# Two edits in a four-stage image kernel: ScalarE takes the first expert and a later copy; residual tiles are loaded, and partly added, during the first sweeps

## The reference, cut to what matters

```python
x = x + dynamic_conv(gn(x))   # 3x3, weights mixed for each sample from 4 experts by a softmax
x = x + scnn_1(gn(x))         # four sweeps of 63 dependent steps
x = x + attention(gn(x))      # linear attention with rotation, plus a 3x3 depthwise conv
x = x + scnn_3(gn(x))         # four sweeps again

# dynamic_conv, for a sample
g = mean(x, (2, 3));  alpha = softmax(relu(g @ w1.T + b1) @ w2.T + b2)
weff = sum_k alpha[k] * experts[k];  out = conv3x3(x, weff) + sum_k alpha[k] * bias[k]

# one sweep (down, up, right, left): row i needs row i - 1
new = row + relu(conv1d(prev, w, b))      # 9 taps, 64 channels to 64
```

## Time and profile before

| what | value |
| --- | --- |
| device time, median of 3 runs | 3130.79 us (3127.74 to 3137.73) |
| the profiled execution's own time | 3132.45 us |
| span of its trace | 3130.7 us |
| mean granted TensorE clock | 0.945 |
| busy: PE, DVE, ACT, POOL | 88%, 69%, 44%, 9% |
| dynamic convolution | 0 to 429 us |
| first sweeps | 429 to 1339 us |
| local part | 1339 to 1583 us |
| attention | 1583 to about 2180 us |
| second sweeps, final sum | to 3067 us, to the end |

### The profile page before, as it was taken

The page is one execution under the profiler, slowest core; times in us unless marked ns, Lnnn a source line. Parts: engine busy times, 40 slices in busy tenths (PEclk is TensorE's granted clock), DMA queues, the critical chain, the costliest instruction groups (busy, mean ns, idle before and its releaser), DMA issues. The chain is left out here.

```text
span 3130.7 us, 71818 instructions
## 1 busy us (share of the span) xinstructions
PE 2747.3 (88%) x25712; PEld 2482.8 (79%) x25712; DVE 2172.1 (69%) x5174; ACT 1363.0 (44%) x2113; POOL 288.4 (9%) x801
## 2 busy tenths in 40 slices
PE   5888879999999999917969998878999999999791
PEld 3666669999999999913447777758999999999791
DVE  7888846666666666687018888886666666666865
ACT  3766642246632222236436666643225662222120
POOL 1112110000000000045000101010000000000602
PEclk9899989999999999958979999998999999999795
DMA  4334230000000000087054877856000000000758
GB/s 89 81 90 99 67 124 0 0 0 0 0 0 0 0 0 0 0 233 198 1 87 73 120 104 102 116 73 107 0 0 0 0 0 0 0 0 0 121 94 127
DMA packets 735622, 164.89 MB, mean 53 GB/s; under 512 B 728209, under 2 KB 728849, under 8 KB 730641
## 3 DMA queue, kind: packets, MB, share of 16 engines
q1 hardware_dynamic: 608928, 136.86, 22.7%
q10 hardware_dynamic: 126576, 26.41, 5.4%
HBM read 96.13 MB, written 67.11 MB: 52 GB/s over the span
## 5 line engine op out<-in xcount | busy, mean ns | idle before, releaser
L269 PE MATMUL L_conv<-L_x_hi,L_w_hi 128*128 128x256 f32 x5040 | 1251.0, 283 | 46.5 <-DVE L_w_lo L236 28.7
L269 PE MATMUL L_conv<-L_x_hi,L_w_lo 128*128 128x256 f32 x5040 | 1249.5, 283 | 0.0
L156 ACT ACTIVATE L_row_b<-S,L_bias 128x256 f32 (+1 forms) x1008 | 514.2, 510 | 1168.9 <-DVE L_x_hi L210 1158.0
L269 PEld LDWEIGHTS L_conv<-L_x_hi,L_w_hi 128*128 128x128 f32 x5040 | 958.7, 190 | 49.5 <-issue 28.9
L269 PEld LDWEIGHTS L_conv<-L_x_hi,L_w_lo 128*128 128x128 f32 x5040 | 957.0, 190 | 0.0
L220 DVE SCALAR_TENSOR_TENSOR S<-L_conv,L_neg_bias,L_row_b 128x256 f32 x1008 | 487.7, 484 | 517.5 <-PE L_conv L273 516.7
L273 PE MATMUL L_conv<-L_x_lo,L_w_hi 128*128 128x256 f32 x5040 | 771.3, 284 | 4.9 <-DVE L_x_lo L212 4.8
L273 PEld LDWEIGHTS L_conv<-L_x_lo,L_w_hi 128*128 128x128 f32 x5040 | 677.7, 190 | 7.4 <-DVE L_x_lo L212 7.4
L212 DVE TENSOR_TENSOR L_x_lo<-S,L_x_hi 128x256 fp32r<-128x256 f32 x1016 | 455.3, 448 | 34.7
L210 DVE TENSOR_SCALAR L_x_hi<-S 128x256 fp32r (+1 forms) x1016 | 316.7, 312 | 35.3
L604 PE MATMUL dc_conv<-dc_xz_hi,dc_w_hi 128*128 128x512 f32 x384 | 171.3, 446 | 6.5 <-DVE dc_w_lo L731 6.5
(11 more groups left out here) (177 smaller groups left out, 2896.4 us busy)
## 6 DMA issues: line engine op xcount, KB each, us to landing
dc_raw<-x SPq DMA_DIRECT2D x32, 512.0 KB, 6.6
x_scratch<-dc_raw SPq DMA_DIRECT2D x16, 1024.0 KB, 7.4
lp_xr<-x_scratch SPq DMA_DIRECT2D x16, 1024.0 KB, 7.0
x_scratch<-lp_xr SPq DMA_DIRECT2D x32, 512.0 KB, 7.7
at_res<-x_scratch SPq DMA_DIRECT2D x32, 512.0 KB, 10.5
x_scratch<-at_res SPq DMA_DIRECT2D x64, 256.0 KB, 5.3
fs_buf<-x_scratch SPq DMA_DIRECT2D x32, 512.0 KB, 6.7
at_G<-x_scratch ACTq DMA_DIRECT2D x56, 256.0 KB, 5.8
```

The source lines that it names most:

```text
L156: nc.scalar.activation(row_b[p][:, :, :], line(k, at_step(k, i), p), ACT.Identity, bias=bias[:, k:k + 1]).then_inc(row_b_ready[p], 1)
L269: nc.tensor.matmul(out, w[:, k, s * P:(s + 1) * P], x_hi[p][:, s:s + J, :], start=(s == 0 and n == 0), stop=False)
```

## The change

**In the dynamic convolution.**
- ACT's fourth copy of a sample into S (`ph` 1, `pw` 1) no longer stands behind the third, but one sample later, behind `evacuate` of the last chunk.
- The product of expert 0 with its weight goes from DVE to ACT (`first_expert`), behind `exps`; `centre` z = 1 now stands ahead of `exps`. Two semaphores are new: `weight_ready` (DVE to ACT), `first_mixed` (ACT to DVE).
- DVE's `remainder` z = 1 goes from behind the mixing to between `mixing_weights` and the mixing.
- At the start, the two expert loads go from ACT's queue to SP's, behind the first sample; low weights of sample 0 are made ahead of its remainders and of the statistics of sample 1; PE does the products of chunks 0 and 1 of sample 0 ahead of the group average of sample 1. At the end, DVE does three of the last four copies and ACT one.

**Behind it.** A class `Shared` owns five tiles of 1 MB. SP loads the x1 of samples 0 to 4 into them in the first sweeps. In the fourth direction POOL adds to each three quarters of S (three times 5 additions of 128x32x16), and DVE takes their 15 statistics between the halves of 15 steps that are written out; the loop of 63 steps becomes four loops and these 15 steps. In the local part only a quarter is left to add for these samples. The band tiles (6 MB) are now loaded on ACT's queue at the start of the local part, and PE waits for them in four parts. SP now loads a sample ahead of storing the next. At the end of the local part, SP loads the constants and the first two `G` tiles into the same five tiles (DVE sets only their edge columns to one), so that the attention starts without these loads, and without the two memsets.

The core of the diff:

```diff
@@ sweeps, DVE @@
-                with dve.Fori(0, STEPS) as i:
-                    for p in range(2):
-                        step(k, dve.snap(i), p)
+                if k == 3 and final:
+                    final.early_vector(dve, step)
+                else: ...
@@ dyn_conv, ACT, sample @@
                     evacuate(n * CH - 1, (k - 1) % PER, CH - 1, n - 1)
+                if not first and not second:
+                    to_slot(n - 2, (k - 2) % PER, 1, 1)
                 if not last:
                     centre(t, k + 1, 0)
                 evacuate(n * CH, k % PER, 0, n)
                 if not last:
                     hidden(n + 1)
+                    centre(t, k + 1, 1)
                     exps(n + 1)
-                    centre(t, k + 1, 1)
+                    first_expert(n + 1)
                 evacuate(n * CH + 1, k % PER, 1, n)
@@ dyn_conv, DVE, sample @@
                     mixing_weights(n + 1)
-                    for e in range(KE):
+                    remainder(n + 1, k + 1, 1)
+                    for e in range(1, KE):
                         mix(n + 1, (k + 1) % 2, e)
...
-                    remainder(n + 1, k + 1, 1)
                     low_weights(n + 1, (k + 1) % 2)
@@ Shared @@
+    def early_pool(self, pool, new_ready, done_before):
+        for n in range(RING):
+            pool.wait_ge(self.x1_in[n], 16)
+        for g in (3, 2, 1):
+            for p in range(2):
+                pool.wait_ge(new_ready[p], done_before(3, STEPS - g * QUARTER))
+            for n in range(RING):
+                self.add_quarter(self.nc.gpsimd, n, g).then_inc(self.quarter_summed, 1)
+    def early_vector(self, dve, step):
...
+        for g in (3, 2, 1):
+            ready = STEPS - g * QUARTER + RING + 1
+            several(at, ready)
+            for n in range(RING):
+                step(3, ready + n, 0)
+                dve.wait_ge(self.quarter_summed, (3 - g) * RING + n + 1)
+                self.quarter_stats(n, g).then_inc(self.early_stats, 1)
+                step(3, ready + n, 1)
+            at = ready + RING
+        several(at, STEPS)
@@ local_part @@
             for n in range(B):
                 sp.wait_ge(x2_ready, n + 1)
+                if n >= 2 and n - 2 + RING < B:
+                    sp.wait_ge(x2_stored[(n - 2) % RING], 32 * ((n - 2) // RING + 1))
+                    sp.wait_ge(normed, n - 1)
+                    shared.load_residual(sp, n - 2 + RING)
                 for q in range(2): ...
+            shared.load_constants(sp, *constants)
+            sp.wait_ge(pads_ready, 4)
+            shared.load_normalised(sp, x2, 0, 0)
+            shared.load_normalised(sp, x2, 1, 1)
@@ local_part, ACT and PE @@
+            bands.load(act)
...
-            pe.wait_ge(bands.loaded, 8 * 16)
             pe.wait_ge(normed, NB)
             for w in range(W):
+                if w % 16 == 0:
+                    pe.wait_ge(bands.loaded[w // 16], 2 * 16)
@@ attention @@
-            for t in G:
-                nc.vector.memset(t[:, :, :], 1.0).then_inc(set_up, 1)
```

More of the change, by code:

```diff
@@ L466, in store @@
                              raw[u][:, :, :].rearrange("p i w -> p (i w)")).then_inc(x1_stored, 16)
-            for n in range(PER):
+            load(0, 0)
+            sp.dma_start(ex[0], halves(experts[:, 0, :])).then_inc(ex_in, 16)
+            sp.dma_start(ex_rest[:, :, :], experts[:, 1:KE, :]).then_inc(ex_in, 16)
+            for n in range(1, PER):
                 load(n, n)
@@ L545, in high_weights, with to_slot @@
                 nc.scalar.copy(halves(w_hi[u][:, :]), w_mix).then_inc(w_hi_ready, 1)
-            def to_slot(n, u, ph):
+            def to_slot(n, u, ph, pw):
                 act.wait_ge(affine_ready, n + 1)
-                for pw in range(2):
-                    dst, src, scale, shift = slot_move(n, u, u % 2, ph, pw)
-                    nc.scalar.activation(dst, src, ACT.Identity, bias=shift, scale=scale).then_inc(s_done, 1)
+                dst, src, scale, shift = slot_move(n, u, u % 2, ph, pw)
+                nc.scalar.activation(dst, src, ACT.Identity, bias=shift, scale=scale).then_inc(s_done, 1)
             def sample(t, k):
@@ L625, in sample @@
                 first, last = isinstance(n, int) and n == 0, isinstance(n, int) and n == B - 1
+                if first:
+                    for q in range(2):
+                        products_high(0, q, 0, 0)
+                        products_high(0, q, 0, 1)
+                        products_low(0, q, 0)
+                    group(1, INP)
+                    products_high(0, 2, 0, 0)
+                    products_high(0, 2, 0, 1)
+                    products_low(0, 2, 0)
+                    hid(1)
+                    products_high(0, 3, 0, 0)
+                    logits(1)
+                    products_high(0, 3, 0, 1)
+                    products_low(0, 3, 0)
+                    return
                 if not last:
@@ L633, in sample @@
                 products_high(n, 1, u, 0)
-                if not first:
-                    group(n - 1, RES)
+                group(n - 1, RES)
                 if not last:
@@ L801, in _ @@
             gate_hidden(0)
-            remainder(0, 0, 0)
             softmax_in(0)
-            remainder(0, 0, 1)
+            mixing_weights(0)
+            dve.wait_ge(ex_in, 2 * 16)
+            for e in range(1, KE):
+                mix(0, 0, e)
+            low_weights(0, 0)
+            for z in range(2):
+                remainder(0, 0, z)
             for q in range(CH):
@@ L820, in _ @@
             dve.wait_ge(affine_ready, B)
-            for pw in range(2):
-                dst, src, scale, shift = slot_move(B - 1, (B - 1) % PER, (B - 1) % 2, 1, pw)
+            for ph, pw in ((0, 1), (1, 0), (1, 1)):
+                dst, src, scale, shift = slot_move(B - 1, (B - 1) % PER, (B - 1) % 2, ph, pw)
                 nc.vector.tensor_scalar(dst, src, scale, shift, ALU.mult, ALU.add)
@@ L831, in __init__, with load @@
         self.band1 = ctx.enter_context(nc.sbuf_tensor("lp_band1", [P, W, HALF], F32))
[L832 to L834 removed]
+        sem = semaphores(nc, ctx, "lpb")
+        self.loaded = [sem(f"loaded{g}") for g in range(4)]
+    def load(self, eng):
         for g in range(4):
             part = slice(g * 16, g * 16 + 16)
[L837 to L838 removed]
@@ L845, with local_part @@
 GROUP_EVERY = 7
 NORM_LAG = 8
-def local_part(nc, ctx, S, bands, affine, x1, x2, group_avg, lepe_b):
+def local_part(nc, ctx, S, bands, affine, shared, x2, group_avg, lepe_b, constants):
     def sb(name, shape, dt=F32):
@@ L854, in local_part @@
     sem = semaphores(nc, ctx, "lp")
-    xr = [sb(f"xr{u}", [P, J, W]) for u in range(RING)]
+    xr, x1_in = shared.xr, shared.x1_in
     avg = sb("avg", [P, P])
@@ L1002, in _ @@
                 if n < B:
-                    mark = front(n)
+                    sums = front(n)
                 if n >= 2:
@@ L1008, in _, with attention @@
                 if n < B:
-                    middle(n, mark)
+                    middle(*sums)
+            dve.wait_ge(normed, B)
+            for u in range(RING):
+                dve.wait_ge(x2_stored[u], 32 * len(range(u, B, RING)))
+            for pad in shared.pads():
+                nc.vector.memset(pad, 1.0).then_inc(pads_ready, 1)
 HEADS, HD = 8, 8
 ROWS = 8
-def attention(nc, ctx, S, affine, x2, x3, consts, rotations, wq_in, wk_in, bq_in, bk_in):
+def attention(nc, ctx, S, affine, shared, x2, x3):
     def sb(name, shape, dt=F32):
@@ L1021, in attention @@
     sem = semaphores(nc, ctx, "at")
-    G = [sb(f"G{u}", [P, J // 2, 2 * W + 2]) for u in range(2)]
-    T = [sb(f"T{u}", [P, J // 2, P]) for u in range(2)]
+    G, rot, cst, wq, wk, b_raw, y = shared.G, shared.rot, shared.cst, shared.wq, shared.wk, shared.b_raw, shared.y
+    g_in, consts_in = shared.g_in, shared.consts_in
+    T = [sb("T0", [P, J // 2, P]), shared.turned]
     res = [sb(f"res{u}", [P, C, J]) for u in range(2)]
@@ L1701, in early_sync, with early_vector, early_pool @@
             self.load(sp, item)
-    def early_pool(self, pool, new_ready, count):
+    def early_vector(self, dve, step):
+        with dve.Fori(0, STEPS) as i:
+            for p in range(2):
+                step(3, dve.snap(i), p)
+    def early_pool(self, pool, new_ready, done_before):
         for p in range(2):
-            pool.wait_ge(new_ready[p], count)
+            pool.wait_ge(new_ready[p], done_before(3, STEPS - PART))
         for item in range(B):
```

214 lines of the change are left out of this document (126 added, 88 removed).

## The result

| kernel | median | runs |
| --- | --- | --- |
| before | 3130.81 us (3126.49 to 3137.73) | 20 |
| changed | 3138.36 us (3132.24 to 3151.82) | 20 |

The ratio of the changed kernel to the one before is 1.0029, with a 95% interval of 1.0021 to 1.0037: slower by 7.5 us by the medians and 9 by the ratio, where 5.8 us faster was forecast. The time lies in the range, but on the other side of no change. The profiled execution's span is 3137.2 us against 3130.7, mean clock 0.941 against 0.945.

The account below looks back on a forecast made before the run. PE bounds the sweeps, a loop between ACT and DVE the dynamic convolution, mainly DVE the local part. Terms 8.7 + 12.0 - 14.0 - 12.5 = -5.8 us against a median of 3130.79 give 3125.0 us, range 3108 to 3142.

Parts of the forecast that it names:

- four terms: Dynamic convolution +8.7, first sweeps +12.0, local part up to the taps -14.0, attention's start -12.5 us; sum -5.8.
- sign that was named for a wrong forecast: Forecast is wrong if the first two terms sum to no loss, or the last two gain less than 20 us.
- Dynamic convolution: Loop between ACT and DVE: cycle becomes 25.0 us; cycles, turns, start and end together cost +8.7 us.
- the two turns: Dynamic convolution: stalls at the loop's turns, covered less in a longer cycle, 0.5 us for each of two: +1.0.
- The end: Dynamic convolution: two copies no longer precede the last evacuation, and the last moves take less: 5.7 us earlier.
- Rival 2: Dynamic convolution: DVE's own work, not the loop with ACT, bounds it; -15.7 instead of +8.7, 3100.6 us; chance 0.10.
- First sweeps: Fourth direction: POOL's 15 additions hold DVE, 4.0 us lost in each of three rounds: +12.0 us.
- Rival 3: First sweeps: POOL's quarter additions take 2.95 us each like whole ones; +31 instead of +12, 3144 us; chance 0.10.
- rival 4: Fourth direction: code loading at seven new seams stalls DVE; +9.7 us, 3134.7 us; chance 0.09.
- Local part: Up to the taps: bands share the DMA engines with loads and stores, transfers bind; the taps come 14.0 us earlier.
- rival 1: Local part: transfers do not bind, bands and stores overlap better; -9.8 us more, 3115.2 us; chance 0.18.
- Attention's start: Constants and first tiles land ahead, leaving DVE's bias preparation as the wait; PE's first transpose comes 12.5 us earlier.

Follow-up runs that it names:

- e1: Changed kernel with 32 bytes per partition left free ahead of the attention's own tiles: 3130.2 us, ratio 0.9998 to the kernel before.
- e7: Kernel before with the residual part of the change alone, plus 32 free bytes ahead of the attention's tiles: 3119.5 us, ratio 0.9961.
- e2: Kernel before with 32 bytes left free ahead of the attention's tiles: 3146.0 us, ratio 1.0040.
- e12: Kernel before with 64 bytes left free ahead of the attention's tiles: 3144.5 us, ratio 1.0039.
- e5: Kernel before with the dynamic convolution's edits alone, except the remainder of z = 1 back behind the mixing: 3127.9 us, ratio 0.9985.
- e3: Kernel before with the dynamic convolution's edits alone: 3143.0 us, ratio 1.0027.
- e10: As e8, with e5's convolution edits, first-chunk statistics behind the mixing weights, and POOL's additions started two steps apart: 3094.8 us, ratio 0.9889.
- e11: As e10, but POOL's 15 quarter additions in the first sweeps left out instead of spaced: 3094.3 us, ratio 0.9881.
- e8: As e7, but six of the bands' eight transfers issued only behind the eighth normalisation: 3108.7 us, ratio 0.9929 to the kernel before.

## Why the prediction was wrong, point by point

**The step that failed is one that isn't in the sum: the attention behind its start was taken as unchanged.** The change adds tiles of 8192, 8320 and 480 bytes ahead of the attention's own, the last of them the five samples' statistics (`sh_bn`). With it the residual tiles begin 96 bytes past a multiple of 128. They are loaded and stored in pieces of 128 bytes (12.59 MB in 98880 packets), and those then take a quarter more of the DMA engines' time (64.3% against 51.1% for the same packets). e1 and e7 take 8.1 us away with 32 free bytes, e2 and e12 put 12 to 14 us on the kernel before. That is shown. Without this cost the change stands at e1's 3130.2, still 5.2 over the forecast, and no change against the kernel before.

The Trainium skill ("DMA: Bandwidth & Descriptors", How a descriptor splits into AXI transactions) has each piece cut at addresses that are multiples of 256 bytes. By that rule, on which the prediction did not draw and whose transactions no trace here shows, pieces of 128 bytes in a tile at a multiple of 128 are never cut, and in one that begins 32, 64 or 96 bytes past it every second piece becomes two transactions; a shift by 128 or 256 changes nothing. The seven programs agree with it in which are slow.

How a busier DMA costs PE time stays open. Some 6 of the 11.6 us are waits of PE that end with nothing the trace shows: all four slow programs have more of them than any of the twelve others. The same DMA engines serve a queue that the trace calls "instruction" (0.41 MB in the window of 176 us), so instructions that come late are a possible cause; no run here tests it, and the rest of the loss has no cause that was found.

That the four terms together came near their sum is luck. They gave -3.0 where -5.8 was forecast, but only because +2.9, -4.5, +4.3 and +0.1 nearly cancel. Neither sign that was named for a wrong forecast appeared: the first two terms were a loss (19.1), and the last two gained over 20 (22.1). Both signs look at the terms of the sum, and none at a stage that the sum leaves out.

**Dynamic convolution: right in mechanism, 2.9 short.** A cycle without a turn is 25.03 to 25.13, but for the first, against the 25.0 forecast, and the wait of the cast for the mixing is still there; e5 shows that it is the remainder's place alone. The casts of samples 2 and 15 lie 25.24 apart each, +13.1 in place of +11.1: half of the 2.0 are the two turns, 26.4 and 25.7 instead of 25.5 (26.2 and 26.3 in e3), half the eleven other cycles, 25.09 on average instead of 25.0. One reading behind the term was wrong: the 24.23 of the kernel before does not hold stalls at the turns alone. Its turns take 25.6 and 25.7, but its other cycles vary from 23.6 to 24.8 and average 23.97. The end gave 4.6 for 5.7; the start cost 3.1 for 3.3. Rival 2 is refuted: DVE's wait for ACT rose from 0.28 to 2.15.

**First sweeps: +7.5 for +12.0.** The period of a quarter addition is 1.6 us, not 1.25 + 0.44 = 1.69, and that is a small part of it. The picture behind the 1.69 was wrong, too: DVE's instruction does not stand between two additions, it lasts as long as the addition beside it. The sum mis-sized what a round gives back: DVE's lead over PE, which my formula left at nothing, absorbs about a microsecond of each round (five periods less 4.45 would be 3.6, measured 2.5). e10 makes use of it five times a round. That this lead is what absorbs it is read from e10, not measured by itself. Rival 3 (2.95 each) and rival 4 (seams) are refuted, the latter by e11, which keeps the seams and has a stage no longer than the kernel before (908.5 against 910.2). The Trainium skill ("GPSIMD Engine Reference", section 3.1) has 4497 ns for an fp32 addition of 2048 elements, from which 1.12 us was estimated for such an addition; the trace has 1.57 to 1.72 beside a busy DVE, and the measurement decides.

**Local part: -9.7 for -14.0.** That transfers bind it was right, and the sixth sample's addition waited for one. Mis-sized were the stores, at 5.2 us each. The 7.7 for a store with its load doesn't follow from the earlier trace rows: 2.10 MB at 253 GB/s are 8.3, so a store is 5.8, six take 3.6 more, and the term would have been -10.4, near the measured -9.7. The trace shows how it came about: beside the bands the first store took SP 17.0. Behind it SP's round of load and store, 8.1 to 8.5, is a little longer than DVE's 7.8 and never catches up. With the bands out of the way, in e8, the transfers bind no more, and the 65.8 us to the taps come near the 62 of rival 1.

**Attention's start: right**, -12.4 for -12.5, with DVE's bias preparation as the last wait.

The range (3108 to 3142) held the time only since it took in most of rival 3's loss; the loss that came was another one.

## What to carry to other kernels

When a change adds or moves tiles in SBUF, compute where the tiles with transfers behind them now begin, before you sum the parts: the cost stands in a stage that the diff doesn't touch. An operation moved "into a free place" has to be put on the cycle between engines first; the remainder was free behind the mixing, and ahead of it it made the cycle 1.4 us longer (25.04 in e3 against 23.65 in e5), its 2.45 less the wait of 0.97 that it hid. Work on POOL beside a loop that DVE feeds should be spread by DVE's lead over PE, not bunched.

## What the runs showed of the hardware

- Transfers in pieces of 128 bytes to and from SBUF tiles that begin 32, 64 or 96 bytes past a multiple of 128 kept the DMA engines busy for a quarter more time than on a multiple (64.3% against 51.1% for the same 98880 packets; share of all queues 0.87 to 0.91 against 0.75), at 32, 64 and 96 alike, and a load of 512 KB landed in 12.7 to 12.8 us instead of 10.8 to 11.1.
- Eight large loads on ACT's queue (6.3 MB) held up SP's issue of two stores (of 512 KB each) for 17.0 us; with 1.6 MB in their place it was 8.2.
- A POOL addition of 128x512 holds each of DVE's SBUF-only instructions for as long as it runs (1.66 for 0.43, 1.10 for 0.29), but not DVE's sum that reads PSUM (0.47).
